# A clamp put into the int8 quantisation of the last layer, on VectorE

## The reference

```
xf = (x5 - mean) * rstd                     # layer norm of the residual stream
a  = max(|xf|) + 1e-8
q  = round(xf / a * 127)                    # whole numbers from -127 to 127
out = x5 + (q @ ternary(W)) * a * scale(W) / 127
```

## Time and profile before

| | us |
|---|---|
| three runs | 3978.52, 3983.03, 3986.02 |
| median | 3983.03 |
| profiled execution | 3978.52 |
| its span | 3976.9 |

### The profile page before, as it was taken

How to read it: one execution, slowest core, us unless ns; L and a number is a source line. 1 busy time by engine, 2 the same in 40 slices (tenths; PEclk the granted TensorE clock), 3 DMA queues, 4 the chain that set the end, 5 groups by cost and what they waited for, 6 DMA issues and landing times.

```text
span 3976.9 us, 119353 instructions
## 1 busy us (share of the span) xinstructions
PE 3722.4 (94%) x34582; PEld 2904.4 (73%) x34583; DVE 3050.0 (77%) x8728; ACT 2790.8 (70%) x8434; POOL 2518.4 (63%) x3252
## 2 busy tenths in 40 slices
PE   5999999999999999979978999999999999999997
PEld 4888888888888888867765666666666666666664
DVE  5888888888888888854546777777777777777775
ACT  4787788888878888844436677776767676766764
POOL 4556566666666666632236777777777777777774
PEclk9999999999999999979989999999999999999998
DMA  4434433333333333324431110111111111101110
GB/s 134 134 112 133 133 111 116 117 117 116 103 111 118 119 102 112 117 70 144 144 101 31 30 36 29 34 32 32 34 31 35 31 35 30 36 28 32 34 30 17
DMA packets 222649, 304.22 MB, mean 76 GB/s; under 512 B 57216, under 2 KB 176256, under 8 KB 222592
## 3 DMA queue, kind: packets, MB, share of 16 engines
q1 hardware_dynamic: 197632, 249.83, 19.9%
q0 software_dynamic: 19200, 52.45, 4.1%
q10 hardware_dynamic: 5760, 1.24, 0.2%
HBM read 239.18 MB, written 64.23 MB: 76 GB/s over the span
## 4 chain that ended last, share of the span: by engine, by line
PE 38%; issue 22%; DVE 14%; POOL 11%; ACT 10%; DVEq 2%; DMA 1%; ACTq 1%; POOLq 1%; SPq 0%
PE Q L1553 10%; PE Q L1546 7%; PE Q L1558 5%; PE Q L1933 3%; PE Q L1779 3%; POOL arena L673 3%; PE Q L1587 2%; DVE mx L1135 2%; PE Q L1791 2%; POOL arena L681 2%; ACT arena L1348 2%; PE Q L1874 2%; ACT arena L1345 1%; POOL arena L678 1%; ACT arena L1342 1%
## 5 line engine op out<-in xcount | busy, mean ns | idle before, releaser
L1558 PE MATMUL Q<-ident,arena 128*128 128x128 f32 x3488 | 581.6, 283 | 104.4 <-ACT arena L1282 35.4
L1558 PEld LDWEIGHTS Q<-ident,arena 128*128 128x128 f32 x3488 | 404.2, 142 | 342.1 <-issue 166.3
L1553 PE MATMUL Q<-Wkvl,arena 128*128 128x512 f32 x1024 | 519.9, 600 | 1.0 <-ACT arena L1497 0.8
L673 POOL TENSOR_TENSOR arena<-arena 128x1024 f32<-128x1024 f32 x256 | 481.5, 1902 | 38.5 <-DMA arena<-cum_rows 37.9
L744 POOL TENSOR_TENSOR l<-l,half_pow 128x8 f32<-128x8 f32 x192 | 317.5, 1653 | 123.3 <-DVE l L1154 123.2
L1466 ACT ACTIVATE arena<-Q,mx 128x128 f32<-128x128 f32 x1024 | 358.8, 385 | 6.5 <-DVE mx L1135 6.2
L1381 ACT ACTIVATE arena<-Q,mx 128x128 f32<-128x128 f32 x1024 | 286.4, 385 | 97.0 <-DVE mx L960 92.8
L1546 PE MATMUL Q<-arena,Win 128*128 128x128 f32 x2560 | 347.8, 280 | 1.1 <-DVE arena L890 1.1
L1587 PE MATMUL Q<-ident,arena 128*128 128x128 f32 x2048 | 320.0, 280 | 23.2 <-ACT arena L1381 13.1
L1546 PEld LDWEIGHTS Q<-arena,Win 128*128 128x128 f32 x2560 | 323.8, 196 | 6.2 <-DVE arena L890 1.9
L914 DVE TENSOR_TENSOR arena<-arena,Q 128x1024 f32<-128x1024 f32 x256 | 311.7, 1218 | 11.1 <-ACT arena L1336 4.3
(11 more groups left out here) (291 smaller groups left out, 10143.0 us busy)
## 6 DMA issues: line engine op xcount, KB each, us to landing
arena<-cum_rows SPq DMA_DIRECT2D x256, 512.0 KB, 6.3
arena<-routed_rows SPq DMA_DIRECT2D x144, 128.0 KB, 2.0
expert_rows<-arena POOLq DMA_DIRECT2D x144, 128.0 KB, 2.0
arena<-in_x_dram SPq DMA_DIRECT2D x128, 128.0 KB, 4.3
arena<-in_ctx_dram SPq DMA_DIRECT2D x128, 128.0 KB, 3.1
x_rows<-arena SPq DMA_DIRECT2D x128, 128.0 KB, 1.7
arena<-x_rows SPq DMA_DIRECT2D x128, 128.0 KB, 2.1
out_dram<-arena SPq DMA_DIRECT2D x64, 128.0 KB, 1.7
```

Of the source, the lines that this page charges most:

```text
L673: tell(g.tensor_tensor(E8[j], E8[j], cums[:, 8 * j:8 * j + 8].unsqueeze(2).broadcast_to([P, 8, T]), ALU.subtract), "diff")
L1553: last = mm(out, lhs(c), rhs(c), start=c == 0, stop=c == n - 1)
L1558: last = nc.tensor.transpose(out[:, c * P:(c + 1) * P], src[:, c * P:(c + 1) * P], ident[:, :])
```

## The change

The scaled values are clamped to the interval from -128 to 127 before they are rounded, by one more instruction in place on xf. The product with the weight's scale moves from behind the reciprocal to behind the clamp. The reciprocal's completion is now waited for at once, and the wait of the clamp stands ahead of the moved product; the rounding has no wait of its own any more. The table `links` gives the number of own waits of a chain, 6 where it was 5.

```
-        links = {... "U_DVE": 5,
+        links = {... "U_DVE": 6,
...
                 J(v.tensor_reduce(am[:, 0:1], xf, AX.X, ALU.max, apply_absolute_value=True))
                 J(v.tensor_scalar(am[:, 0:1], am[:, 0:1], Q_EPS, None, ALU.add))
-                cue("U_DVE", v.reciprocal(am[:, 1:2], am[:, 0:1]))
+                J(v.reciprocal(am[:, 1:2], am[:, 0:1]))
+                J(v.tensor_scalar(xf, xf, am[:, 1:2], 127.0, ALU.mult, ALU.mult))
+                J(v.tensor_scalar(xf, xf, 127.0, -128.0, ALU.min, ALU.max))
                 v.tensor_scalar(am[:, 2:3], am[:, 0:1], wscale[:, 3:4], None, ALU.mult)
-                heed(dve, "U_DVE", b)
-                J(v.tensor_scalar(xf, xf, am[:, 1:2], 127.0, ALU.mult, ALU.mult))
                 tell(v.tensor_scalar(aq[:, :], xf, ROUND, ROUND, ALU.add, ALU.subtract), "aq")
```

More of the change, by code:

```diff
@@ L362, in two_layers @@
         signals("U", "POOL", "ln7_rstd", after="F")
-        links = {"M_DVE": 1, "D_DVE": 13, "V_DVE": 2, "W_DVE": 1, "P_DVE": 2, "F_DVE": 3, "G_DVE": 4, "A_DVE": 2, "C_DVE": 1, "K_DVE": 2, "T_DVE": 1, "U_DVE": 5,
+        links = {"M_DVE": 1, "D_DVE": 13, "V_DVE": 2, "W_DVE": 1, "P_DVE": 2, "F_DVE": 3, "G_DVE": 4, "A_DVE": 2, "C_DVE": 1, "K_DVE": 2, "T_DVE": 1, "U_DVE": 6,
                  "M_POOL": 2, "W_POOL": 2, "F_POOL": 2, "A_POOL": 1, "C_POOL": 2, "K_POOL": 3, "H_POOL": 1, "T_POOL": 1, "U_POOL": 1}
```

## The result

| | before | after |
|---|---|---|
| time, us (median, 5 runs each) | 3983.03 (3978.52 to 3993.43) | 4018.83 (4011.28 to 4025.66) |
| ratio, 95% interval | | 1.0084 [1.0065, 1.0103] |
| profiled execution, span | 3976.9 | 4027.1 |
| median distance between two roundings | 28.77 | 29.23 |

The forecast was 4011, with 4002 to 4030. 64 x 0.44 us is a ratio of 1.0070, inside the measured interval. On another chip the same two kernels took the same time as each other, and most of the experiments are about why.

What follows compares the result with a forecast made beforehand. The prediction took DVE's unbroken run (11 of 28.8 us a round) as the bound, despite PE's 96%. 64 x 0.44 = 28 us on the profiled 3978.5 gave 4006.7, or 4011 from the median 3983.0; range 4002 to 4030.

Steps and rivals of the forecast that it cites:

- Step 1: Reciprocal to scaling: moving the product away gains 0, since the reciprocal's completion sets the scaling's start; 0.09 us at most.
- Step 2: The added clamp on DVE alone takes 0.29 us, with 0.42 as upper bound.
- Step 3: Clamp and rounding beside GpSimd's second gather: the clamp takes over the stall at 0.53 us, the rounding falls to 0.29.
- Rival A: At the gather, the clamp is not held: 0.29 or 0.42 us, giving 3997 or 4005 us; chance 8%.
- Step 4: Scaling to L1135 in a loop round grows from 0.84 to 1.28 us: 0.44 more, bounds 0.42 and 0.57.
- Step 5: In the drain, without a gather, the block grows from 0.60 to 1.04 us, again 0.44.
- What hides none of it: Behind the block up to L1159, DVE has no wait on another engine that could cover the added 0.44 us.
- rival D: At the transposes of kn, PE's own matmuls set the round and cover the clamp: not slower, 3985 us; chance 4%.
- Rival B: The rounding falls behind GpSimd's pow and stands to its end: 0.92 us a round, 4039 us; chance 6%.
- Rival C: At the loop's head, the mask instruction loses its race with GpSimd's L771: 51 us on top, 4062; chance 8%.

Runs made afterwards that it cites:

- two_clamps: The changed kernel with the clamp written twice, on the second chip: 4048.85 us, ratio 1.0010 to the kernel before.
- four_clamps: The changed kernel with the clamp written four times in a row, on the fourth chip: 4080.10 us, ratio 1.0222 to the kernel before.
- move_only: The kernel before with only the product moved, between scaling and rounding, no clamp, on the second chip: 4038.07 us, ratio 0.9981.
- swap_room_after: The changed kernel with L1154 ahead of L1135 and the mask row, ln7 statistics and Kln5 moved, fourth chip: 3980.56 us, ratio 0.9962 to the kernel before.
- before_same: The kernel before, unchanged, run again on the third chip: 4056.01 us, ratio 0.9998.
- idle_clamp: The kernel before with one clamp that alters no value, put where DVE waits ahead of L1128, second chip: 4044.61 us, ratio 1.0006.
- the pair with the swap: The kernel before and the changed one, both with L1154 moved ahead of L1135, on the fourth chip: 3988.93 and 4020.00 us.
- swap_before: The kernel before with the step of L1154 moved ahead of the first maximum L1135, on the fourth chip: 3988.93 us, ratio 0.9997.

## Why the prediction was right, and where it was not

**Step 1, the product leaves the reciprocal: 0.** Right: 0.20 to the scaling in both.

**Step 2, the clamp alone: 0.29.** Right: 0.29 in the drain, in two_clamps and in four_clamps, 0.33 from start to start.

**Step 3, the stall is handed on.** Right: 0.53 on the clamp, 0.28 on the rounding. move_only and swap_room_after show that the stall goes by where the instruction lies against the gather, not by which instruction it is. Rival A is out.

**Step 4, a round: 0.44.** Measured 0.457. Of the terms, clamp to product came to 0.564 in the median where 0.57 was said, product to rounding to 0.131 instead of 0.11, rounding to L1135 to 0.199 instead of 0.21. L1135 itself takes 0.684 where it took 0.672. Each is off by 0.02 at most. Step 5, the drain: 1.05 for 1.04. One sum of the prediction is off: 0.42 and 0.57 us in 64 rounds, with the 4 us of scatter, give 4006 to 4024 and not 4004 to 4022. The range of 4002 to 4030 holds both.

**What hides none of it.** Right on the first and the fourth chip, not so on the second and third. The text named the cover that it would take, a wait of DVE behind the block, and found none in the trace. On two chips this very wait is there. This is rival D in its effect (the change costs nothing because PE sets the round) but not by its mechanism: its price rested on PE's 0.24 before the transposes of kn, and that wait stood on all chips (0.29 in before_same). What moved was PE's strips, ahead of L1135. The trace of one chip could not have shown it. What it could have shown is how thin the margin was: PE stands idle 0.35 us between the end of its strips and the transposes of aq, so L1135, which needs those strips, would wait as soon as they took some 0.35 us longer.

**Rival B** is disproved by two_clamps. The Trainium skill ("SBUF — State Buffer", section "Who interferes with whom") would have the rounding wait for a GpSimd instruction that already runs. The traces agree for the mask instruction against L771 (1.12 here) and not for one column of pow (0.28, inside 0.62). They agree as well for the clamp of idle_clamp, which started inside one L771 and ended 0.15 us after it. **Rival C** is there in single rounds and costs about 2 us more than before, not 51.

**The sum.** 28 us forecast, 36 between the medians, the interval of the ratio being 26 to 41 us, and 31 in the pair with the swap. The forecast of 4011 is 8 us below the median measured: the profiles put 1 us of that on the round and about 5 on single late rounds and the drain, and the rest is within the scatter of the runs.

Left open: why PE's strips pause beside the gather on two of the chips and not on the others. The granted clock of the stretch from 2300 to 3850 us was 1.00 in all profiles, so the clock does not tell. PE's supply of instructions suggests itself, since the pauses are put down to "issue". The Trainium skill ("Runtime: NRT & Kernel Launch", section "Instruction fetch mechanics") says that each engine's sequencer fetches its own instructions in blocks while it executes, and that this is mostly hidden. The traces do not bear that out as the cause: the two instruction queues moved 29 or 30 and 28 to 30 packets in a whole profile and none at all between 2300 and 3850 us, on either kind of chip. The chips were also measured one after the other, so what is called a kind of chip here could be a state of it. The kernel before is 1.3 to 1.8% slower on those chips (53 to 74 us), and 0.84 x 64 = 54 us are the strips' share of the rounds.

## What to carry to other kernels

Where an engine runs a chain without waits, price an added instruction from start to start, and move a known stall to whichever instruction lands in its place. Rounds that differ by chance are free experiments on what sets the round. But a cost that rests on two engines meeting within some tenths of a microsecond need not hold on the next chip: here the same edit was worth 0.8% at first and 0.7% on the fourth chip, and nothing on the third, and only the kernel before, run again beside it, showed which kind of chip it was. And when an engine pauses for no wait that the profile names, look for the rounds without the pause and see what else is missing in them: here it was another engine's gather.

## What the runs showed of the hardware

- **The end of a gather holds DVE.** A quick DVE instruction (0.29 us on 256 columns) that starts with 0.42 us of GpSimd's indirect gather left takes 0.53, with 0.30 left 0.41, with 0.24 left 0.35, with 0.20 left 0.30: it ends 0.10 after the gather. With 0.48 left it takes 0.28 (swap_room_after). The edge is sharp: in swap_before eight roundings that started 0.519 to 0.528 us into the gather took 0.29, and seven of their rounds were 0.23 us shorter (28.55; the eighth had a late mask instruction); 45 that started 0.527 us in or later took 0.53. Read from these rows, what matters is not that the two overlap but whether DVE is still busy some 0.14 us before the gather ends.
- **A one-column instruction of GpSimd does not hold DVE, a 128x512 one does**: 0.28 for a rounding inside the one-column pow (two_clamps), but 1.03 for a clamp beside L771 (idle_clamp), where an unheld one takes 0.29. The pow itself gets longer, 0.68 in the changed kernel where it took 0.57.
- **On some chips PE pauses in a burst of small weight loads beside GpSimd's gather**: 48 loads in 0.97 us on the first and fourth chip, in 2.1 us on the second and third. The pauses end 0.6 and 1.35 us after the gather's start, move with it, and are absent where it is absent; the clock is the same and the instruction queues are silent.
